# Slot-attention steps on one Trainium2 core: one-element activations ahead of the table switches, and a bias product moved behind the up product

## The reference, cut to what matters

```python
for _ in range(T):                       # T = 3
    prev = slots
    q = _ln(slots, lnq_g, lnq_b) @ wq + bq
    logits = jnp.einsum('bnd,bkd->bnk', k, q) / scale
    attn = jax.nn.softmax(logits, axis=-1) + EPS_ATTN
    attn = attn / jnp.sum(attn, axis=1, keepdims=True)
    upd = jnp.einsum('bnk,bnd->bkd', attn, v)
    slots = upd @ wu + bu + prev
    h = _ln(slots, lnm_g, lnm_b) @ w1 + b1
    slots = jax.nn.gelu(h, approximate=False) @ w2 + b2 + slots
    slots = _ln(slots + x_cls[:, None, :], lnp_g, lnp_b)
```

## Time and profile before

| what | value |
|---|---|
| median of 3 runs | 2439.63 us |
| lowest and highest of them | 2437.85 and 2439.83 us |
| the profiled execution's own time | 2435.36 us |
| its span (first to last instruction) | 2433.6 us |
| mean granted clock of TensorE | 0.919 of full speed |
| busy, share of the span | PE 83%, DVE 69%, ACT 63%, POOL 36% |
| the slot steps in the span | from about 45 us to 216 us, some 56 us for a step |

### The profile page before, as it was taken

One profiled execution on the slowest core, in us unless ns is written; L12 is line 12 of the kernel. 1 busy time (PEld: TensorE's weight loads), 2 busy tenths in 40 slices (PEclk: granted clock), 3 DMA queues, 4 the chain that ended last, 5 costly groups with the idle time before them and its releaser, 6 DMA issues.

```text
span 2433.6 us, 38335 instructions
## 1 busy us (share of the span) xinstructions
PE 2031.6 (83%) x14062; PEld 894.9 (37%) x14066; DVE 1689.8 (69%) x3124; ACT 1537.7 (63%) x1937; POOL 865.7 (36%) x1354
## 2 busy tenths in 40 slices
PE   2654799926889999999999999999999999988651
PEld 1332576711223333333433333333333333333321
DVE  6776211136678888888878888788878888886456
ACT  1432233303568888788778887888788878868442
POOL 4443000012234435434444344344443444433331
PEclk9776899966899999999999999999999999999665
DMA  1000101032133344332253334432353334321100
GB/s 48 1 0 1 35 1 34 0 78 56 38 65 82 80 89 84 80 88 67 68 91 88 81 82 79 92 75 61 70 108 88 74 74 93 84 54 36 32 6 9
DMA packets 148642, 144.40 MB, mean 59 GB/s; under 512 B 30887, under 2 KB 136163, under 8 KB 148451
## 3 DMA queue, kind: packets, MB, share of 16 engines
q1 hardware_dynamic: 148463, 142.05, 26.2%
HBM read 79.01 MB, written 60.51 MB: 57 GB/s over the span
## 4 chain that ended last, share of the span: by engine, by line
PE 56%; DVE 14%; ACT 4%; issue 3%; POOL 1%; DMA 1%; SPq 0%; POOLq 0%; DVEq 0%; ACTq 0%
PE ps L1265 14%; PE ps L1229 7%; PE ps L1218 6%; DVE smax L1763 6%; PE ps L1343 5%; PE ps L1384 4%; PE ps L1375 4%; PE ps L1277 4%; ACT big L1498 2%; PE ps L1318 2%; DVE rot L1779 2%; PE ps L1302 2%; PE ps L1240 1%; PE ps L1252 1%; PE ps L1335 1%
## 5 line engine op out<-in xcount | busy, mean ns | idle before, releaser
L1498 ACT ACTIVATE big<-ps 128x1024 f32<-128x1024 f32 x960 | 955.5, 1026 | 262.3 <-PE ps L1229 243.1
L1763 DVE TENSOR_REDUCE smax<-ps 128x2 f32<-128x1024 f32 x768 | 921.7, 1221 | 266.7 <-PE ps L1218 261.1
L1265 PE MATMUL ps<-big,vaug 128*32 128x512 f32 x3072 | 412.4, 615 | 2.9 <-ACT big L1498 2.9
L1218 PE MATMUL ps<-k,q 49*128 49x512 bf16 x1536 | 296.8, 395 | 63.7 <-DVE smax L1763 33.7
L1229 PE MATMUL ps<-q,k 52*128 52x512 bf16 x1536 | 296.5, 388 | 11.2 <-DVE smax L1763 5.4
L1694 POOL CAST mparts<-smax 128x16 bf16<-128x16 f32 x96 | 19.4, 202 | 578.1 <-DVE smax L1763 578.1
L1218 PEld LDWEIGHTS ps<-k,q 49*128 49x128 bf16 x1536 | 73.1, 94 | 313.5 <-DVE smax L1763 105.0
L694 DVE SCALAR_TENSOR_TENSOR state<-ps,share,state 128x128 f32<-128x128 f32 x128 | 36.0, 344 | 200.3 <-PE ps L665 200.3
L682 ACT ACTIVATE big<-ps 128x512 f32<-128x512 f32 x128 | 76.5, 598 | 142.9 <-PE ps L656 142.9
L1770 DVE TENSOR_REDUCE maxima<-ps 128x8 f32<-128x616 f32 x192 | 144.6, 794 | 30.7 <-PE ps L1252 29.1
L1343 PE MATMUL ps<-xnT,w 128*128 128x512 f32 x288 | 164.9, 658 | 0.9 <-ACT xnT L1535 0.9
(11 more groups left out here) (290 smaller groups left out, 3026.7 us busy)
## 6 DMA issues: line engine op xcount, KB each, us to landing
q<-scratch_queries SPq DMA_DIRECT2D x48, 384.0 KB, 6.3
k<-scratch_keys SPq DMA_DIRECT2D x48, 384.0 KB
cq<-scratch_cross_queries SPq DMA_DIRECT2D x48, 384.0 KB, 5.8
scratch_queries<-rparts SPq DMA_DIRECT2D x24, 384.0 KB, 2.4
scratch_keys<-rparts SPq DMA_DIRECT2D x24, 384.0 KB, 2.6
scratch_cross_queries<-rparts SPq DMA_DIRECT2D x24, 384.0 KB, 2.5
scratch_queries<-rparts SPq DMA_DIRECT2D x24, 256.0 KB, 2.7
scratch_keys<-rparts SPq DMA_DIRECT2D x24, 256.0 KB, 3.0
```

The lines of the kernel that those rows point to most:

```text
L1218: last = nc.tensor.matmul(out[:, u], m.q6[rows, v % 2, 2 * g + pr, qt * P:(qt + 1) * P], m.k6[rows, v % 2, 2 * g + pr, :], start=True, sto ...
L1265: last = nc.tensor.matmul(m.ps[32 * j:32 * j + 32, pv_bank, :], of_head(m.vaug, v % 2 * TB + kt, g, j), of_quad("self", q)[:, j, :], start ...
L1498: nc.scalar.activation(of_quad(kind, p // 2)[:, p % 2 * 2:p % 2 * 2 + 2, :], banks("exp" if kind == "self" else "cross exp", p), ACT.Exp, ...
L1763: nc.vector.tensor_reduce(m.smax[:, n % 2, qt, :, pr], banks("max", i), AX.X, ALU.max).then_inc(s_read["self"], 1)
```

## The change

ACT's program gets one-element activations (partition 0, one element in, one element out, into a tile that nothing reads): of Exp ahead of step 0, of Gelu behind the exponentials of every step, of Exp behind the gelus of steps 0 and 1. In PE's program the condition's product leaves `down(s, b)` and is issued right behind the up product, in `up(s, b)`. One tile of one float32 per partition is added.

```diff
             def up(s, b):
                 pe.wait_ge(in_m, count(s, b))
                 nc.tensor.matmul(m.ps[:, 2 * b + 1, :], m.mats0[:, 4, :], m.xnT[:, b, :], start=True, stop=True).then_inc(h_ps, 1)
+                nc.tensor.matmul(m.ps[:, 2 * b, :], m.ones32[0:1, :], m.cond_rows[0:1, b:b + 1, :].to_broadcast([1, TB, D]),
+                                 start=True, stop=False)

             def down(s, b):
                 pe.wait_ge(h_sb, count(s, b))
-                nc.tensor.matmul(m.ps[:, 2 * b, :], m.ones32[0:1, :], m.cond_rows[0:1, b:b + 1, :].to_broadcast([1, TB, D]),
-                                 start=True, stop=False)
                 for t in range(TB):
...
+            def load_table(function):
+                nc.scalar.activation(m.unused[0:1, :], m.minus_half[0:1, 0:1], function)
+
...
+            load_table(ACT.Exp)
             for s in range(SLOT_STEPS):
                 for k in range(B + 2):
...
                     if k >= 2:
                         exponentials(s, k - 2)
+                load_table(ACT.Gelu)
                 for k in range(B + 2):
...
                     if k >= 2:
                         gelu(s, k - 2)
+                if s + 1 < SLOT_STEPS:
+                    load_table(ACT.Exp)
...
         m.minus_half = sb("minus_half", [P, TB])
+        m.unused = sb("unused", [P, 1])
```

## The result

The changed kernel takes 2452.99 us (median of 5, 2441.02 to 2456.88) against 2437.85 us (5 runs, 2431.71 to 2439.83): a ratio of 1.0051, 95% interval 1.0032 to 1.0071 (the ratios of this document are estimates over all runs and not quotients of two medians, which would be 1.0062 here). It is **slower by 0.5%**, about 12 us, where 2 us and "no measurable change" were forecast, and the median lies above the range. Measured once more beside the last experiments, with 12 runs, the ratio is 1.0041 (1.0019 to 1.0063); those 12 times fall into two groups, eight from 2433.84 to 2445.27 and four from 2452.62 to 2458.80.

The account below looks back on a forecast made before the run. PE, full from turn 1 to down 1, was taken to bound each step; -0.3 us for Exp and +2.4 for PE (Gelu's 0.76 included) gave +2.1 on 2439.63, so 2441.7 us, range 2436.5 to 2445.0.

Parts of the forecast that it names:

- What bounds the step: Slot steps: PE is full from turn 1 to down 1; a step ends about 20 us behind down 1.
- Gelu loads, 0.76 us: Three table loads ahead of ACT's first gelu, mostly hidden by up 1: worth 0.76 us together, not 3 x 1.28.
- Exp loads, 0.3 us: Two table loads ahead of the first exponential in steps 1 and 2: removing them saves 0.3 us in all.
- Rival A: MLP half: clock rises 2.5 us sooner, Gelu load lies on the path; -0.1 a step, -0.6 in all, 2439.0; chance 0.22.
- The drain of 1.38 us: ACT's table switches: the skill's extra drain would make five worth 13.3 us; the prediction took the extra as nothing.
- The moved product, +2.4 us: PE's queue: one more condition's product ahead of down 1, less vanished idle time; +0.91, +0.57, +0.91 us by step.
- The aside that turn 2 would end at about 80.3: PE's queue behind cond 0: turn 2 ends at about 80.3, gain 2 about a microsecond later; no new wait for ACT.
- Rival C: Next halves: later step ends tip PE bursts into longer half-clock stretches, 1.2 us each; +8.1 us, 2447.7; chance 0.09.

Follow-up runs that it names:

- the kernel before, held: Unread products of 128 rows by 512 columns put into PE's idle time of the slot steps, against the kernel before: 2434.07 us, ratio 1.0005.
- second profile: Profile of the changed kernel measured once more, nothing else altered: profiled execution 2433.84 us, median 2440.92 us, ratio to before 1.0041.
- first profile: Profile of the changed kernel's first measurement, against the kernel before: profiled execution 2447.78 us, median 2452.99 us, ratio 1.0051.
- after with 128 rows: The changed kernel with the condition's product over all 128 contraction rows, weights of 1/128, same place behind up: 2430.94 us, ratio to before 0.9980.

## Why the prediction was wrong, point by point

- **What bounds the step** was right. Down 1 releases add_output 1, and the next step's first turn follows 19.76 us behind it, before (105.83 - 86.07) and after (112.67 - 92.91). The loss came ahead of it: POOL's root 1 is still released by DVE, but after 5.22 us of idle time and not about 2.
- **Gelu loads, 0.76 us; Exp loads, 0.3 us** were small, as forecast: ScalarE's edit alone gives 0.9992. Their exact size isn't shown, since 1.26 of the 1.7 us that the stage gained come with an earlier rise of the clock in step 2. That up 1 hid the load was right for a low clock, and Rival A's remark that at full clock it lies bare was right too: PE idles 0.87 us for the gelu behind the load in the kernel before, held, and the moved product then costs nothing (10.00 us with and without it). Its price of the pair of edits at full clock, -0.1 us a step, was too small: 12.60, 13.62 and 12.61 us became 10.00, because with the bare load the clock fell too.
- **The drain of 1.38 us** that the Trainium skill's page gives ("ScalarE: Activation LUTs", section "What ACT_TABLE_LOAD costs"): five loads taken off ScalarE's busy stretches brought at most 1.7 us in the stage, not 13.3, and the new loads end 0.02 us ahead of the next activation (65.06 + 1.28 against 66.36).
- **The moved product, +2.4 us, is the term that failed.** Its step was "this assumes that a product at half clock costs twice; the total of PE's work before down 1 then matters and not its order". The first part was right (2.00 us against 1.05). The second took the moment of the rise as given. But what PE is given at half clock moves that moment: 5.5 us behind turn 1 became 8.1 in the mild case and 18.9 in the worst one. The term measures 7.2 us (second profile, 40.48 - 33.30) to 16.4 us (first profile) in place of 2.4. (The aside that turn 2 would end at about 80.3 is 0.3 below its own terms, 74.99 + 0.91 + 1.71 + 2.10 + 0.89 = 80.60; nothing rests on it.)
- **Rival C** had the right resource, a longer stretch at half clock, and a wrong mechanism: not the later start of a burst, but the one-row product inside it. Its 8.1 us would have been nearer to the measured 12, but only by luck, since the delay that it adds up is not the one that came. Having put it down to chance phases is what left it a chance of 0.09.
- I had the clue in view. Rows 3 show that the stretch before the rise, 74.99 to 80.35, holds turns and up products alone, of 128 rows each, and the edit puts the only instruction of another kind into it.

## What to carry to other kernels

Look at what PE does in the stretch before its clock rises, and keep products of one contraction row out of it (no count between 1 and 128 was tried): here one of them per sequence held the clock at 1.2 GHz for 3 to 13 us more, though PE was busy throughout. A bias or condition added by a one-row product is better spread over all 128 rows with weights of 1/128, at either of the two places tried; in down, and with the table loads in idle time, it made this kernel 0.4% faster than before. And a load that PE's slow clock hides is bare when the clock is high, so the two are to be judged together.

## What the runs showed of the hardware that was not expected

- PE busy at 1.00 in every window is not enough for the clock to rise: with one-row products in the stretch it stayed at 0.50 for 18.9 us behind turn 1, with 128-row products in the same places it rose 4.5 to 6.1 us behind turn 1 in all six halves (79.4 against 74.46 and 81.1 against 75.30 in step 0).
- Rows of zero weights do as well as others: 0.9978 against 0.9980.
- The clock can fall while PE is busy without a break, behind two one-row products close together (granted clock 0.58 in the window from 86 to 87, PE busy 1.00). Once down it can stay down for 17 us of busy PE (138.2 to 155.2 in the kernel before, held).
- A product of 512 columns over one row occupies more of PE than one over 128 rows, from start to start: 1.05 us at full clock (84.88 - 83.83) and 2.00 at half, against 0.86 (81.65 to 82.51, after with 128 rows) and 1.71 (77.91 to 79.62).
